# First attention: VectorE multiplies the output of two pairs back ahead of head 0's remainder; GpSimd's gates become semaphore increments

## The chip, the cores and the metric

The kernel runs on one core of a Trainium2 chip. The metric is the device time of one execution in microseconds (us), the median of several. The engines are TensorE (PE in the profile), VectorE (DVE), ScalarE (ACT), GpSimd (POOL) and SyncE (SP), which here only issues DMAs. Each takes its instructions from a queue of its own in order, and they meet only at semaphores.

## The reference

Two transformer layers in a row over `x` of 8 x 512 x 128 float32, each an attention and a mixture-of-experts network, with a layer norm after each of the four. Only the first attention is touched by the change:

```python
q, k, v = jnp.einsum('bsx,xAnh->Abnsh', input, w)      # 16 heads of 64
q = q + q_bias[:, None, :]
a = jnp.einsum('bnqh,bnkh->bnqk', q, k) * h ** (-0.5)
emb = jnp.einsum('sf,fnh->nsh', sins, positional * FREQS ** (-0.5))
pos_scores = jnp.einsum('bnqh,nvh->bnqv', q, emb) * h ** (-0.5)
a = a + relative_causal(pos_scores)
a = jax.nn.softmax(jnp.where(mask, a, NEG_INF), axis=-1)
o = jnp.einsum('bnqk,bnkh->bqnh', a, v).reshape(b, s, n * h)
out = o @ (out_kernel * (fan_in * fan_out) ** (-0.25)) + out_bias
x = _layernorm(x + out, axis=-1)
```

## The kernel before

The four parts of the program follow one another: first attention (`rel_attention_phase`, some 60 to 765 us), expert network, second attention, second expert network. The first attention walks over 8 batches and, in each, over 8 pairs of heads; `n` counts the 64 pairs, `p` is the pair in its batch, `b` the batch, `k` the parity of the pair, `h` the head in the pair. `schedule` writes the same order of pairs out for every engine: pairs 0, 1, 2 and 7 of a batch by themselves, 3 to 6 in a loop. Each engine has a `body` for a pair, and its order is written by hand; so what follows an instruction on its engine waits behind it.

To keep float32 precision with 16-bit matmuls, operands are split: a high half in float16, and a low half that is the remainder. What happens for pair `n`:

- **q and k.** TensorE projects them into PSUM; VectorE brings q out (`q_evac`, L624), ScalarE k (`k_copy`, L586). GpSimd splits each in `split` (L703): a gate (`pool_gate`, L130), a select that writes the high half (L705), and, behind a wait for that select, a subtraction that writes the low half (L708). It does so four times in a pair, `k` and `q` of head 0, then of head 1. The gate adds two constants in a column of its own that no one reads. It is the instruction that stands behind the waits for semaphores and ahead of the select. The select counts `pool_steps` up by one, and the wait inside `split` is for that count to reach `chain_n`.
- **Scores.** TensorE forms them in three PSUM banks (L483 to L486), VectorE takes the negated row maxima (`maxima`, L606), ScalarE the exponentials with their sums (`exps`, L565). The bank of head 0 is free for head 1 when ScalarE has read it, and the other way round.
- **Weights.** ScalarE writes the high half of the exponentials (`high`, L574), VectorE the remainder (`low`, L618: two inputs in SBUF, 128x1280). A DMA from SP's queue turns both round (`turn`, L406) once `low` is done.
- **Sums.** VectorE takes reciprocals (L614); SP stores them and spreads them over partitions (`store_r`, `spread_r`).
- **Output.** Two pairs later TensorE multiplies the turned weights by v (`weighted_values(n - 2)`, L502) into `pv_ps`. VectorE multiplies the result by the reciprocals into `o32` (`normalise(n - 2)`, L632; it waits for that product, for the reciprocals' DMA and for the projection before), and TensorE projects `o32` into the batch's sum (`project_out`, L519).

TensorE's order in a pair is: scores of head 0, projections of k, q and v for later use, `weighted_values(n - 2)`, scores of head 1, projection of q, `project_out(n - 2)`. ScalarE's is: `exps(0)` with `k_copy` inside, `high(0)`, the high half of v, `exps(1)`, `high(1)`. In pair 2 of a batch VectorE adds the batch before to its input (`batch_sum`) and takes its statistics (`batch_stats`), GpSimd then the reciprocal root (L136, L137); in pair 7 VectorE adds a bias (L642) and normalises (L123).

VectorE's order in a pair is the part that the change touches, with GpSimd's `split`; both are printed here.

Of the kernel before, what the change touches and what calls it, by code (L numbers as in the profile page):

```python
# [22 lines left out]
P = 128  # L23
# [104 lines left out]
def pool_gate(nc, m, rows, at=0):  # L128

    nc.gpsimd.tensor_tensor(m.gate[rows, at:at + 1], m.mhalf[rows, 0:1], m.mhalf[rows, 1:2], ALU.add)  # L130
# [154 lines left out]
def rel_attention_phase(nc, io, m):  # L285


    with ExitStack() as ctx:
# [5 lines left out]
        q32 = [sb(f"q32_{h}", [P, S], F32) for h in range(2)]  # L294
        q_h = [sb(f"q_h{h}", [P, S], F16) for h in range(2)]
        q_l = [sb(f"q_l{h}", [P, S], F16) for h in range(2)]
        k32 = sb("k32", [P, S], F32)
# [21 lines left out]
        q_mm, q_out, q_split = pair("q_mm"), pair("q_out"), pair("q_split")  # L319
        k_mm, k_out, k_split = sem("k_mm"), sem("k_out"), pair("k_split")  # L320
# [6 lines left out]
        pool_steps, turn_open = sem("ra_pool"), sem("turn_open")  # L327
# [272 lines left out]
        @block.vector  # L600
        def _(dve):
            def maxima(h, n):
                for u in range(3):
                    dve.wait_ge(s_mm[h], count(n, u))
                    for c, col in UNIT_CHUNKS[u]:
                        ins = nc.vector.tensor_reduce(nmax[h][:, c:c + 1], score_ps[u][:, col:col + P * (c + 1)],  # L606
                                                      AX.X, ALU.max, negate=True)
                    ins.then_inc(max_done[h], 1)

            def reciprocals(h, n, k):  # L610
                dve.wait_ge(exp_done[h], count(n, 2))
                if later(n, 2):
                    dve.wait_ge(r_stored, 32 * (n - 1))
                nc.vector.reciprocal(rsum[h][k][:, :], sums[h][:, :]).then_inc(r_done[h], 1)  # L614

            def low(h, n, k):
                dve.wait_ge(p_hi[h], n + 1)
                nc.vector.scalar_tensor_tensor(p16[h][k][:, 1, :], prob[h][:, :], P_SCALE, p16[h][k][:, 0, :],  # L618
                                               ALU.mult, ALU.subtract).then_inc(p_lo[h], 1)

            def q_evac(h, n, pw):
                dve.wait_ge(q_mm[h], n + 1)
                dve.wait_ge(q_split[h], n)
                nc.vector.scalar_tensor_tensor(q32[h][:, :], q_ps[:, :], m_flat(m.q_bias)[:, ds(PAIRS * h + pw, 1)],  # L624
                                               m.q_mult[:, h, :], ALU.add, ALU.mult).then_inc(q_out[h], 1)

            def normalise(n, k):
                dve.wait_ge(pv_mm, n + 1)
                dve.wait_ge(r_in, 32 * (n + 1))
                if later(n, 1):  # L630
                    dve.wait_ge(out_mm, n)
                nc.vector.tensor_tensor(o32[:, :].rearrange("p (c q) -> p c q", q=P), pv_ps[:, :].rearrange("p (c q) -> p c q", q=P),  # L632
                                        r_bc[k][:, :].rearrange("p (q c) -> p c q", c=QC), ALU.mult).then_inc(o_done, 1)

            def v_low(n, k):
                dve.wait_ge(v_hi, n + 1)
                nc.vector.scalar_tensor_tensor(v_l[k][:, :, :].rearrange("p c n -> p (c n)"), v_ps[:, :], W_SCALE,
                                               v_h[k][:, :, :].rearrange("p c n -> p (c n)"), ALU.mult, ALU.subtract).then_inc(v_lo, 1)

            def add_bias(b):  # L640
                xb = m_flat(m.x)[:, ds(b * S, S)].rearrange("p (c d) -> p c d", d=D)
                nc.vector.tensor_tensor(xb, xb, m.bo_bc[:, :].unsqueeze(1).to_broadcast([P, QC, D]), ALU.add).then_inc(bias_in, 1)  # L642

            def batch_sum(b):
                dve.wait_ge(out_mm, PAIRS * (b + 1))
                dve.wait_ge(bias_in, b + 1)
                dve.wait_ge(ln_dve, b + 1)
                nc.vector.scalar_tensor_tensor(y[:, :, :].rearrange("p c d -> p (c d)"), out_ps[:, :], O_SCALE / P_SCALE,
                                               m_flat(m.x)[:, ds(b * S, S)], ALU.mult, ALU.add).then_inc(y_done, 1)

            def batch_stats(b):
                dve.wait_ge(y_done, b + 1)
                layer_norm_stats(nc, dve, m, b, y, st, mv)

            def batch_norm(b):
                layer_norm_apply(nc, dve, m, b, y, mv, rstd,
                                 m_flat(m.x)[:, ds(b * S, S)].rearrange("p (c d) -> p c d", d=D)).then_inc(ln_dve, 1)

            def body(n, t, b, p, k):
                wrap = at(p, PAIRS - 1)  # L660
                behind = wrap and not at(b, 0)
                pw = 0 if wrap else p + 1
                maxima(0, n)
                if at(p, 2) and not at(b, 0):
                    batch_sum(b - 1)
                if later(n, 1):
                    reciprocals(1, n - 1, 1 - k)
                    low(1, n - 1, 1 - k)
                q_evac(0, n + 1, pw)
                if at(p, 2) and not at(b, 0):  # L670
                    batch_stats(b - 1)
                reciprocals(0, n, k)
                low(0, n, k)
                if later(n, 2):
                    normalise(n - 2, k)
                maxima(1, n)
                q_evac(1, n + 1, pw)
                v_low(n, k)
                if wrap:
                    add_bias(b)  # L680
                if behind:
                    batch_norm(b - 1)

            def first_front():
                vector_gate(nc, m).then_inc(ln_dve, 1)
                q_evac(0, 0, 0)
                q_evac(1, 0, 0)

            def last():
                n = B * PAIRS  # L690
                reciprocals(1, n - 1, 1)
                low(1, n - 1, 1)
                normalise(n - 2, 0)
                normalise(n - 1, 1)
                batch_sum(B - 1)
                batch_stats(B - 1)
                batch_norm(B - 1)

            schedule(dve, first_front, body, last)

        @block.gpsimd
        def _(pool):
            def split(rows, src, hi, lo, chain_n):  # L703
                pool_gate(nc, m, rows)
                nc.gpsimd.affine_select(out=hi, in_=src, compare_op=ALU.is_ge, fill=0.0, base=0,  # L705
                                        pattern=[[1, S]], channel_multiplier=0).then_inc(pool_steps, 1)
                pool.wait_ge(pool_steps, chain_n)
                return nc.gpsimd.tensor_tensor(lo, src, hi, ALU.subtract)  # L708


            def split_q(h, n):
                pool.wait_ge(q_out[h], n + 1)
                pool.wait_ge(s_mm[h], 3 * n)
                pool.wait_ge(k_split[h], n + 1)
                split(slice(0, P), q32[h][:, :], q_h[h][:, :], q_l[h][:, :], 4 * n + 2 + 2 * h).then_inc(q_split[h], 1)

            def split_k(h, n):
                if h == 0:
                    pool.wait_ge(k_out, n + 1)
                pool.wait_ge(s_mm[h], 3 * n)  # L720
                pool.wait_ge(q_split[1 - h], n + h)
                r = slice(64 * h, 64 * h + 64)
                split(r, k32[r, :], m.k_h[h][r, :], m.k_l[h][r, :], 4 * n + 1 + 2 * h).then_inc(k_split[h], 1)

            def front(n):
                for h in range(2):
                    split_k(h, n)
                    split_q(h, n)

            def body(n, t, b, p, k):  # L730
                split_k(0, n + 1)
                split_q(0, n + 1)
                split_k(1, n + 1)
                split_q(1, n + 1)
                if at(p, 2) and not at(b, 0):
                    layer_norm_gpsimd(nc, pool, m, b - 1, mv, ve, rstd)

            def last():
                layer_norm_gpsimd(nc, pool, m, B - 1, mv, ve, rstd)

            schedule(pool, lambda: front(0), body, last)
# [1200 lines left out]
def m_flat(t):  # L1942

    a = t[tuple(slice(None) for _ in t.shape)]
    names = "abcd"[:len(t.shape) - 1]
    return a if len(names) == 1 else a.rearrange(f"p {' '.join(names)} -> p ({' '.join(names)})")
# [90 lines left out]
```

## Time and profile before

| | us |
|---|---|
| median of 3 runs | 1633.0 (1631.59 to 1633.61) |
| the profiled execution | 1630.46 |
| its span, first to last instruction | 1628.7 |

Busy time over the whole span: TensorE 1351.0 us (83%), VectorE 1305.7 (80%), ScalarE 947.3 (58%), GpSimd 921.4 (57%). Between 200 and 300 us, in the middle of the first attention, it is TensorE 86.8, VectorE 91.5, ScalarE 70.9, GpSimd 87.5 of 100 us, at a granted clock of 1.00. No engine is full there. In a timeline the columns are start and duration in us, the engine, the line, the operation, output and input with their shapes, and in brackets idle time of the engine just before and what ended it. A start and a duration add up to an end; the next instruction of the engine often starts up to 0.09 us before it.

### The profile page before, as it was taken

The page shows a single profiled execution, that of the slowest core. Times are in us where ns is not written, and L with a number is a line of the kernel's source. Part 1 is how long each engine was busy: PE and PEld are TensorE (multiplying, and loading weights), DVE is VectorE, ACT ScalarE, POOL GpSimd, SP SyncE. Part 2 cuts the span into 40 slices and gives each one's busy share as a digit, 9 for nine tenths or more (in the row PEclk, how much of TensorE's full clock was granted, in tenths as well). Part 3 has the DMA queues.
Part 4 walks back from the last instruction along what each step waited for, and adds up shares of the span by engine and source line. Part 5 has one row for each costly group of instructions (what it writes and reads, how often), then busy time and mean ns, then how long its engine had stood idle before and what let it go on. Part 6 is the DMA issues. An engine that isn't in the chain of part 4 may idle for free. (4 is left out here: it accounts for less than half of the span.)

```text
span 1628.7 us, 36836 instructions
## 1 busy us (share of the span) xinstructions
PE 1351.0 (83%) x11495; PEld 775.6 (48%) x11495; DVE 1305.7 (80%) x2722; ACT 947.3 (58%) x1857; POOL 921.4 (57%) x1203
## 2 busy tenths in 40 slices
PE   4888888888988988886698987489899899997936
PEld 3466656655665656654366665123332333332316
DVE  3799899998999898996788888387777877777834
ACT  2676767776767767773244444157666666665631
POOL 2788988888898989896455555211221231231635
PEclk9899999999999999997699999599999999999978
DMA  5667766565666656564000000411011111101001
GB/s 153 136 152 144 146 145 145 129 154 134 147 145 144 144 139 148 131 147 100 1 1 1 0 0 0 150 48 37 29 35 34 35 32 30 40 27 32 25 8 33
DMA packets 401554, 133.51 MB, mean 82 GB/s; under 512 B 362156, under 2 KB 389793, under 8 KB 401377
## 3 DMA queue, kind: packets, MB, share of 16 engines
q1 hardware_dynamic: 398144, 128.41, 33.2%
q10 hardware_dynamic: 1824, 3.15, 0.6%
q0 software_dynamic: 1536, 1.34, 0.3%
q8 instruction: 26, 0.43, 0.1%
q14 instruction: 24, 0.19, 0.1%
HBM read 37.14 MB, written 13.15 MB: 31 GB/s over the span
## 5 line engine op out<-in xcount | busy, mean ns | idle before, releaser
L565 ACT ACTIVATE prob<-score_ps,nmax 128x512 f32<-128x512 f32 (+3 forms) x512 | 264.8, 525 | 202.7 <-DVE nmax L606 201.9
L1577 DVE TENSOR_REDUCE a_nm<-a_s 128x1 f16<-128x512 f32 x512 | 324.5, 687 | 52.8 <-PE a_s L1349 51.9
L1503 ACT ACTIVATE a_pt<-a_st 128x1024 f32<-128x1024 f32 x256 | 260.7, 1021 | 121.8 <-PE a_st L1367 118.7
L618 DVE SCALAR_TENSOR_TENSOR p<-prob,p 128x1280 f16<-128x1280 f32 x128 | 214.4, 1675 | 44.8 <-ACT p L574 44.8
L1349 PE MATMUL a_s<-a_kop,a_qop 128*128 128x512 f16 x512 | 198.1, 388 | 58.8 <-DVE a_nm L1577 42.3
L606 DVE TENSOR_REDUCE nmax<-score_ps 128x1 f32<-128x512 f32 (+3 forms) x512 | 217.9, 480 | 18.1 <-PE score_ps L486 15.9
L708 POOL TENSOR_TENSOR k_l<-k,k_h 64x512 f16<-64x512 f32 x130 | 191.5, 1473 | 10.9
L483 PE MATMUL score_ps<-k_h,q_h 128*128 128x512 f16 (+3 forms) x512 | 156.5, 306 | 48.5 <-ACT prob L565 28.9
L130 POOL TENSOR_TENSOR gate<-mhalf 128x1 f32<-128x1 f32 (+1 forms) x284 | 85.8, 302 | 190.5 <-ACT k L586 64.4
L708 POOL TENSOR_TENSOR q_l<-q,q_h 128x512 f16<-128x512 f32 x130 | 183.0, 1408 | 10.8
L574 ACT ACTIVATE p<-prob 128x1280 f16<-128x1280 f32 x128 | 162.6, 1271 | 8.5
L902 ACT ACTIVATE hid<-fps,b_cols 128x512 f32<-128x512 f32 x130 | 86.4, 687 | 126.6 <-PE fps L862 126.6
L998 POOL TENSOR_TENSOR hid_l<-hid,hid_h 128x512 f16<-128x512 f32 x65 | 97.1, 1494 | 105.3 <-DVE hid_h L966 105.3
L485 PE MATMUL score_ps<-k_h,q_l 128*128 128x512 f16 (+3 forms) x512 | 155.2, 303 | 0.0
L484 PE MATMUL score_ps<-k_l,q_h 128*128 128x512 f16 (+3 forms) x512 | 155.2, 303 | 0.0
L1367 PE MATMUL a_st<-a_qop,a_kop 128*128 128x512 f16 x512 | 152.1, 380 | 0.2
L1349 PEld LDWEIGHTS a_s<-a_kop,a_qop 128*128 128x128 f16 x512 | 50.5, 99 | 184.4 <-DVE a_nm L1577 151.5
L1380 PE MATMUL a_pv<-a_pt,a_vaug 128*32 128x512 f32 x1024 | 137.2, 608 | 0.7 <-ACT a_pt L1503 0.7
L502 PE MATMUL pv_ps<-pt,v_h 128*64 128x256 f16 (+1 forms) x1536 | 119.1, 259 | 1.9 <-DMA pt<-p 1.9
L1699 POOL TENSOR_TENSOR a_vaug<-a_v,a_bv 128x128 f32<-128x128 f32 x32 | 14.4, 453 | 184.1 <-PE a_pv L1380 129.8
L519 PE MATMUL out_ps<-wo,o 128*128 128x128 f32 (+1 forms) x512 | 76.7, 295 | 50.1 <-DVE o L632 50.1
L486 PE MATMUL score_ps<-causal,ident_bf 128*128 128x128 bf16 x512 | 113.2, 221 | 0.0
(328 smaller groups left out, 3319.2 us busy)
## 6 DMA issues: line engine op xcount, KB each, us to landing
r_bc<-r_parts SPq DMA_DIRECT2D x128, 128.0 KB, 2.8
a_qop<-q_parts SPq DMA_DIRECT2D x32, 128.0 KB
a_kop<-k_parts SPq DMA_DIRECT2D x128, 24.0 KB
x_tok<-in_L_attn_input_dram SPq DMA_DIRECT2D x4, 512.0 KB, 12.4
pt<-p SPq DMA_TRANSPOSE x128, 4.1
r_parts<-rsum SPq DMA_DIRECT2D x128, 2.0 KB, 2.2
e_w<-in_L_ffn_w_dram SPq DMA_DIRECT2D x1, 2048.0 KB, 8.4
q_parts<-a_q_h SPq DMA_DIRECT2D x16, 128.0 KB
```

The lines of the kernel that those rows point to most:

```text
L483: nc.tensor.matmul(o, q_h[h][:, qs], m.k_h[h][:, 0:w], start=True, stop=False)
L484: nc.tensor.matmul(o, q_h[h][:, qs], m.k_l[h][:, 0:w], start=False, stop=False)
L485: nc.tensor.matmul(o, q_l[h][:, qs], m.k_h[h][:, 0:w], start=False, stop=False)
L565: ins = nc.scalar.activation(prob[h][:, P_OFF[c]:P_OFF[c] + w], score_ps[u][:, col:col + w], ACT.Exp, bias=nmax[h][:, c:c + 1], accum_out= ...
L574: nc.scalar.activation(p16[h][k][:, 0, :], prob[h][:, :], ACT.Copy, scale=P_SCALE).then_inc(p_hi[h], 1)
L606: ins = nc.vector.tensor_reduce(nmax[h][:, c:c + 1], score_ps[u][:, col:col + P * (c + 1)], AX.X, ALU.max, negate=True)
L618: nc.vector.scalar_tensor_tensor(p16[h][k][:, 1, :], prob[h][:, :], P_SCALE, p16[h][k][:, 0, :], ALU.mult, ALU.subtract).then_inc(p_lo[h], 1)
L708: return nc.gpsimd.tensor_tensor(lo, src, hi, ALU.subtract)
L1349: nc.tensor.matmul(s_ps[k][:, :], qop[:, g, c * P:(c + 1) * P], kop[:, hh, g, :], start=True, stop=True).then_inc(s_mm[k], 1)
L1367: mm = nc.tensor.matmul(st_ps[r][:, i, :], kop[:, 2 * r + i, g, kc * P:(kc + 1) * P], qop[:, g, :], start=True, stop=True)
L1503: nc.scalar.activation(pt[kc % 2][r][:, :, :], st_ps[r][:, :, :], ACT.Exp, scale=1.0 / SC).then_inc(exp_done[r], 1)
L1577: nc.vector.tensor_reduce(nm[g % 2][:, c, hh:hh + 1], s_ps[c % 2][:, :], AX.X, ALU.max, negate=True).then_inc(max_done[c % 2], 1)
```

## The change

On VectorE `normalise(n - 2, k)` moves from behind `low(0, n, k)` to ahead of it. On GpSimd the gate in `split` is replaced with an increment of the semaphore `pool_steps` that the queue does itself; since every split now adds two to that count, the constants that the splits wait for are doubled. The gates of other parts of the program stay.

```diff
@@ -670,9 +670,9 @@
                 reciprocals(0, n, k)
-                low(0, n, k)
                 if later(n, 2):
                     normalise(n - 2, k)
+                low(0, n, k)
                 maxima(1, n)
@@ -700,8 +700,8 @@
-            def split(rows, src, hi, lo, chain_n):
-                pool_gate(nc, m, rows)
+            def split(src, hi, lo, chain_n):
+                pool.sem_inc(pool_steps, 1)
                 nc.gpsimd.affine_select(out=hi, in_=src, compare_op=ALU.is_ge, fill=0.0, base=0,
                                         pattern=[[1, S]], channel_multiplier=0).then_inc(pool_steps, 1)
                 pool.wait_ge(pool_steps, chain_n)
@@ -712,7 +712,7 @@
-                split(slice(0, P), q32[h][:, :], q_h[h][:, :], q_l[h][:, :], 4 * n + 2 + 2 * h).then_inc(q_split[h], 1)
+                split(q32[h][:, :], q_h[h][:, :], q_l[h][:, :], 8 * n + 4 + 4 * h).then_inc(q_split[h], 1)
@@ -720,7 +720,7 @@
-                split(r, k32[r, :], m.k_h[h][r, :], m.k_l[h][r, :], 4 * n + 1 + 2 * h).then_inc(k_split[h], 1)
+                split(k32[r, :], m.k_h[h][r, :], m.k_l[h][r, :], 8 * n + 2 + 4 * h).then_inc(k_split[h], 1)
```

## Rows read from the trace of the kernel before

**Rows 1.** Waits, 100 to 700 us: total us, times, longest us.

```profile
DVE p L618 <- ACT p L574: 37.1, 47, 0.9
```

**Rows 2.** Timeline, VectorE, one pair late in a batch; columns as above.

```profile
449.26 1.66 DVE L606 TENSOR_REDUCE nmax<-score_ps 128x1 f32<-128x512 f32 x4
...
454.42 1.50 DVE L618 SCALAR_TENSOR_TENSOR p<-prob,p 128x1280 f16<-128x1280 f32 x1
455.84 0.74 DVE L624 SCALAR_TENSOR_TENSOR q<-q_ps,q_bias,q_mult 128x512 f32<-128x512 f32 x1
...
457.50 1.66 DVE L618 SCALAR_TENSOR_TENSOR p<-prob,p 128x1280 f16<-128x1280 f32 x1 [0.85 <-ACT p L574]
459.09 1.06 DVE L632 TENSOR_TENSOR o<-pv_ps,r_bc 128x512 f32<-128x512 f32 x1
460.08 1.66 DVE L606 TENSOR_REDUCE nmax<-score_ps 128x1 f32<-128x512 f32 x4
```

**Rows 3.** Timeline, ScalarE, the same pair.

```profile
453.32 0.67 ACT L565 ACTIVATE prob<-score_ps,nmax 128x512 f32<-128x512 f32 x1
...
456.20 1.27 ACT L574 ACTIVATE p<-prob 128x1280 f16<-128x1280 f32 x1
```

**Rows 4.** Timeline, GpSimd, the same pair.

```profile
450.36 1.16 POOL L708 TENSOR_TENSOR q_l<-q,q_h 128x512 f16<-128x512 f32 x1
451.66 0.19 POOL L130 TENSOR_TENSOR gate<-mhalf 64x1 f32<-64x1 f32 x1
451.80 0.61 POOL L705 TENSOR_SCALAR_AFFINE_SELECT k_h<-k 64x512 f16<-64x512 f32 x1
...
453.96 0.61 POOL L705 TENSOR_SCALAR_AFFINE_SELECT q_h<-q 128x512 f16<-128x512 f32 x1
454.65 2.28 POOL L708 TENSOR_TENSOR q_l<-q,q_h 128x512 f16<-128x512 f32 x1
...
457.21 0.60 POOL L705 TENSOR_SCALAR_AFFINE_SELECT k_h<-k 64x512 f16<-64x512 f32 x1
```

**Rows 5.** Timeline, TensorE, the same pair: first score, last of `weighted_values`.

```profile
451.65 0.39 PE L483 MATMUL score_ps<-k_h,q_h 128*128 128x512 f16 x1 [1.02 <-ACT prob L565]
...
457.18 0.22 PE L502 MATMUL pv_ps<-pt,v_h 128*64 128x128 f16 x2
```

**Rows 6.** Timeline, all engines, an early pair of a batch.

```profile
405.26 1.05 DVE L632 TENSOR_TENSOR o<-pv_ps,r_bc 128x512 f32<-128x512 f32 x1
...
410.76 2.08 DVE L618 SCALAR_TENSOR_TENSOR p<-prob,p 128x1280 f16<-128x1280 f32 x1
...
412.68 0.20 POOL L130 TENSOR_TENSOR gate<-mhalf 64x1 f32<-64x1 f32 x1 [1.20 <-ACT k L586]
...
413.52 0.22 PE L502 MATMUL pv_ps<-pt,v_h 128*64 128x128 f16 x2
...
414.25 1.78 DVE L618 SCALAR_TENSOR_TENSOR p<-prob,p 128x1280 f16<-128x1280 f32 x1 [0.67 <-ACT p L574]
...
414.85 1.23 POOL L130 TENSOR_TENSOR gate<-mhalf 128x1 f32<-128x1 f32 x1 [0.17 <-POOL k_l L708]
...
415.95 1.06 DVE L632 TENSOR_TENSOR o<-pv_ps,r_bc 128x512 f32<-128x512 f32 x1
```

**Rows 7.** Timeline, VectorE, change of batch and the third pair behind it.

```profile
479.15 1.67 DVE L618 SCALAR_TENSOR_TENSOR p<-prob,p 128x1280 f16<-128x1280 f32 x1 [0.84 <-ACT p L574]
...
485.36 2.24 DVE L123 TENSOR_SCALAR x_tok<-ln_y,ln_mv,ln_rstd 128x128 f32 x4
487.52 1.67 DVE L606 TENSOR_REDUCE nmax<-score_ps 128x1 f32<-128x512 f32 x4
...
492.28 1.69 DVE L618 SCALAR_TENSOR_TENSOR p<-prob,p 128x1280 f16<-128x1280 f32 x1 [0.88 <-ACT p L574]
...
512.74 0.86 DVE L110 BATCH_NORM_STATS2 ln_st<-ln_y 128x6 f32<-128x128 f32 x4
```

**Rows 8.** Timeline, SP's queue: the transpose of head 1's weights.

```profile
456.01 2.60 SPq L406 DMA_TRANSPOSE pt<-p  x1
```

## The prediction

> **What bounds the kernel now.** I read three views, in this order: the groups of instructions and the waits of the stretch 100 to 700 us, then the timeline of one pair on each engine, then the pairs around a change of batch. The first attention has 64 pairs, so its 700 us are some 10.8 us a pair. A pair is taken here from one `maxima(0)` on VectorE to the next.
>
> The waits show idle time of VectorE before head 0's `low`: 37.1 us in 47 pairs, 0.8 in each, until ScalarE's high half is there [rows 1]. The timeline shows the in-order chain behind it: `low(0)` at 457.50, `normalise` at 459.09, `maxima(1)` at 460.08 [rows 2]. `maxima(1)` lets ScalarE go on with `exps(1)`, `high(1)`, `exps(0)`, `k_copy`, `high(0)`, which lets `low(0)` of the next pair go. So the 0.98 us of `normalise` (460.08 less 459.09) lie inside a ring ScalarE - VectorE. Its ScalarE part from `exps(0)` at 453.32 to the end of `high(0)` at 457.47 is 4.15 us [rows 3].
>
> A second ring is just as long. On GpSimd a pair is four splits: gate, select, subtract. An undisturbed one takes 2.16 us (select at 451.80 to select at 453.96), the other kind 3.25 (453.96 to 457.21), because its subtract takes 2.28 us and not 1.16 [rows 4]. The long ones lie exactly over VectorE's two `low`: the subtract issued at 454.65 ends at 456.93, which is 1.15 us after 455.78, and VectorE goes on to its next instruction at 455.84 [rows 2, 4]. So the two engines exclude one another: whichever is running a `low` or a split operation makes the other wait. Two short and two long splits are 10.82 us, the whole pair (`maxima(1)` at 449.26 and at 460.08), and in this part of the batch GpSimd never idles. TensorE's first score of the pair (451.65) starts 0.14 us after the subtract issued at 450.36 ends at 451.52 [rows 4, 5].
>
> At the start of a batch, and in all of the first one, the picture differs. GpSimd waits 1.20 us for `k_copy`, VectorE's `low(1)` falls into that idle time and pays for it with 2.08 us against 1.50, and from `normalise` at 405.26 to the next at 415.95 are 10.69 us [rows 6]. Between batches a pair takes 13.13 us (479.15 to 492.28), since the bias and the normalisation (2.24 us) come in [rows 7]. A batch is 88.6 us: by `maxima(1)` 13.13, 10.69, 10.80, 10.69 and four of 10.83.
>
> **The change part by part.**
>
> *Gates.* Four gates a pair go; each sits between the semaphore it waits for and its select, and costs the select 0.14 us (451.66 to 451.80) [rows 4]. In its place stands an increment that the queue must still run through. Bounds: nothing below, and 0.14 us above, where it costs what the gate did. The nearest row is SP's: `low(1)` ends at 455.92, and the transpose behind a wait and an increment starts at 456.01, so wait and increment together take 0.09 us [rows 2, 8]. I take 0.04, a saving of 0.10 a split and 0.4 a pair, 0 to 0.56. The Trainium skill ("Advanced Engine Details and Errata", DMA Bandwidth Details) gives a semaphore increment about one cycle on trn2; by that the saving would be 0.14 a split, an estimate, and the pair 0.16 us shorter than in my sum. No row here shows an increment alone.
>
> A gate can also be the instruction that takes the wait: 1.23 us at 414.85, where 0.19 is usual [rows 4, 6]. I book no gain for that 1.0 us. The gate waits there for VectorE's `low`, and the select behind it then meets the same `low`. The Trainium skill ("SBUF — State Buffer", SBUF: two separate sides) states the exclusion as a lock held for a full instruction, between a VectorE operation with two SBUF inputs and any GpSimd operation that reads SBUF; by it the select, with one input, waits too, and this part is worth nothing. No row here shows a select waiting for a `low`, so the other outcome is the first rival.
>
> *The move.* `normalise(n-2)` now comes before `low(0)`. It needs the product of two pairs back, whose last matmul is issued at 457.18 and ends at 457.40. VectorE is free for it at 456.6 (`low(1)` 454.42, the q evacuation at 455.84, the reciprocals) [rows 2, 5]. So in the steady pairs it starts at 457.43 and not in the idle time, and `low(0)`, queued behind it, starts at 458.41 instead of 457.50. That is 0.91 us later, and with it `maxima(1)` comes no earlier, measured from the first score: the 0.98 us leave the ring and a wait of nearly the same size for TensorE takes its place. Who waits behind: ScalarE's `exps(1)`, SP's transpose of head 0 (its queue has nothing else to do then), and TensorE's projection, which gets its input 1.7 us earlier and did not need it. At the start of a batch the product ends at 413.74, and VectorE is free at 413.58 (0.67 before 414.25) [rows 6], so there the cover is nearly right, and right after a change of batch it is complete.
>
> *The new pair.* Count from the end of head 0's subtract. TensorE starts at 0.13, its product ends at 5.90 (5.75 from 451.65 to 457.40) [rows 5]; `normalise` 5.9 to 6.9; `low(0)` from 6.9. GpSimd: each split 2.05 without its gate, so `low(1)`, at 2.90 as now (454.42 less 451.52), meets the boundary between q1's select and subtract (2.9), and `low(0)` lands in the next subtract (6.3 to 7.4) or its end. A `low` occupies 1.35 us (454.42 to 455.78). If it comes within an instruction of GpSimd the pair pays 1.0 to 1.13 (2.28 less 1.15), since the hand-over is hidden; in a gap 1.35. The pair is thus 4 x 2.05 = 8.2 plus 2.1 to 2.3: 10.3 to 10.5. I take 10.4.
>
> The ring through the new wait: 5.77 (to the end of the product) + 0.98 + `low(0)` 1.4 + 1.4 for the first maximum and the first exponential (0.67 [rows 3], the maximum about the same), together 9.6, plus what `low(0)` waits for GpSimd, at most 1.04 (a subtract just issued). That is at most 10.6, under today's 10.83. ScalarE's ring is today's 10.82 less the 0.98 that leaves it, 9.8, and may wait as long; where it does, it too ends at 10.7.
>
> *Batch change.* From `maxima(0)` after the normalisation (487.52) to `low(0)` the time is ScalarE's, and the 0.88 us of idle time take the moved instruction nearly whole. The pair goes from 13.13 to 12.1 [rows 7]: a gain of 1.0. In the third pair of a batch, `batch_sum` and `batch_stats` stand before it (512.74 on) and fill VectorE already [rows 7]; there `normalise` is only moved. With GpSimd now running closer behind, its two `low` can be blocked by 0.4 and 0.8 us where they meet nothing today: 0 to 1.4 worse, I take 0.9.
>
> *Sum.* A batch: -1.0 (change), +0.9 (third pair), and for six pairs (two of 10.69, four of 10.83, together 64.7) against 6 x 10.4 = 62.4: -2.3. Net -2.4, times 7 is -17. The first batch has no normalisation: 6 pairs from 10.70 to 10.4, -2. With rounding, -18. The profiled execution took 1630.5 us (span 1628.7 and 1.8 around it), 2.5 below the median of 1633.0; its 1612.5 stand for a median of 1615. The ends of the unknowns: pair 10.25 and third pair unharmed give -30, 1603; pair 10.6 and third pair +1.4 give -5, 1628.
>
> **The rivals.**
>
> *More comes back (chance 0.12).* If a select may run beside a `low`, head 0's `low` costs GpSimd some 0.3 and not 1.0, GpSimd falls under 9.9, and the rings of 9.6 to 10.0 decide: pair 10.0. Six pairs give -4.7, with the change of batch -5.7, times 7, and the first batch -4: about -42 with the third pair at its dearer end left out, 1591. For it: no select in these rows is long. Against it: the `low(0)` of 457.50 took 1.66 us, as if it waited for the select that ran from 457.21 to 457.81 [rows 2, 4].
>
> *The gates were not the price (0.12).* The increment and its dispatch cost what the gate did. GpSimd still needs 10.8 a pair and the moved 0.98 only turns into waits for TensorE and GpSimd. Left are -7 (batch changes) and +6 (third pairs): 1632. For it: the gate's 0.14 is dispatch, and an increment is dispatched too.
>
> *Slower (0.10).* `low(0)` now waits for `normalise`, hence for TensorE, and both `low` start in GpSimd's gaps, so each costs 1.35 instead of 1.13. That is +0.4 a pair; it decides once the gates give back less than this 0.4. With nothing given back, 48 pairs x 0.4 = 19, +10 for the third pairs, -7 for the batch changes, and the median is 1655; half way it is 1645. Against it: a `low` that starts in one gap shifts GpSimd so that the next one seldom does.
>
> **How the numbers follow.** My forecast, GpSimd-bound pairs of 10.4 us, has 0.66: 1615, own range 1603 to 1628. A measurement of this kernel can tell 0.2% from no change, 3.3 us, so the forecast and the first rival count as faster, 0.78 in all; no difference 0.12; slower 0.10. The range of 8 in 10 leaves out most of the first rival and of the slower one: 1600 to 1636.
>
> **What would show it.** Right: no gate rows; steady pairs of 10.3 to 10.5; GpSimd without idle time in nearly all pairs, the first batch included; a new wait of VectorE at `normalise` for TensorE's product, 0.3 to 0.9 us, in the place of the one at `low`; TensorE's projection no longer waiting for `normalise`; the pair at the change of batch near 12.1. Wrong: selects of 1.2 to 1.9 us that nevertheless leave 10.8 a pair, or selects unblocked beside a `low` and pairs near 10.0; the gap between subtract and select still 0.3 us (an increment as dear as the gate); `low(0)` above 2.5 us each time.

## The result

| | before | after |
|---|---|---|
| median of 12 runs each, one chip, us | 1631.39 | 1633.85 |
| ratio of after to before, 95% interval | | 1.0021 (1.0012 to 1.0029) |
| the same two kernels on another chip, 20 and 10 runs | 1632.08 | 1632.08, ratio 1.0005 (0.9994 to 1.0016) |
| span of the profiled execution | 1628.7 | 1630.1 |

The change gains nothing; on the first chip the median is 2.5 us longer. The forecast was 1615 us, 18 us less than the 1633.0 known then. Ratios here and below leave out runs that the chip slowed down; there was one, of the kernel with the third pair in the old order, at 1968 us and a mean clock of 0.65.

Where the time went is seen best pair by pair. In what follows a pair is the time between two remainders of v on VectorE (`v_low`, one in each pair), and p is its place in the batch. These are the pairs of the fifth batch, in us:

| pair | 0 | 1 | 2 | 3 | 4 | 5 | 6 | 7 | batch |
|---|---|---|---|---|---|---|---|---|---|
| before | 13.13 | 10.69 | 10.80 | 10.70 | 10.84 | 10.82 | 10.81 | 10.84 | 88.6 |
| forecast | 12.1 | 10.4 | 11.7 | 10.4 | 10.4 | 10.4 | 10.4 | 10.4 | 86.2 |
| after | 12.85 | 10.37 | 12.34 | 12.22 | 9.97 | 10.45 | 10.36 | 10.45 | 89.0 |

Six of the eight pairs became shorter, as forecast. Pairs 2 and 3 (the third and fourth of a batch) lost 1.5 us each, and that used up the whole gain. From the first to the last such mark the first attention took 696.3 us before and 697.8 after.

**Steady pairs.** Steady pairs are those late in a batch, where one pair is like the next. VectorE, after (timeline; columns as in the rows ahead of the prediction):

```profile
464.49 1.76 DVE L606 TENSOR_REDUCE nmax<-score_ps 128x1 f32<-128x512 f32 x4
...
466.25 1.46 DVE L618 SCALAR_TENSOR_TENSOR p<-prob,p 128x1280 f16<-128x1280 f32 x1
...
469.28 1.08 DVE L632 TENSOR_TENSOR o<-pv_ps,r_bc 128x512 f32<-128x512 f32 x1 [0.66 <-PE pv_ps L502]
470.28 1.80 DVE L618 SCALAR_TENSOR_TENSOR p<-prob,p 128x1280 f16<-128x1280 f32 x1
472.00 1.67 DVE L606 TENSOR_REDUCE nmax<-score_ps 128x1 f32<-128x512 f32 x4
```

GpSimd in the same pair:

```profile
465.69 0.61 POOL L705 TENSOR_SCALAR_AFFINE_SELECT q_h<-q 128x512 f16<-128x512 f32 x1 [0.26 <-POOL k_l L708]
466.39 2.34 POOL L708 TENSOR_TENSOR q_l<-q,q_h 128x512 f16<-128x512 f32 x1
468.89 0.60 POOL L705 TENSOR_SCALAR_AFFINE_SELECT k_h<-k 64x512 f16<-64x512 f32 x1 [0.16 <-POOL q_l L708]
469.57 1.15 POOL L708 TENSOR_TENSOR k_l<-k,k_h 64x512 f16<-64x512 f32 x1
470.99 1.56 POOL L705 TENSOR_SCALAR_AFFINE_SELECT q_h<-q 128x512 f16<-128x512 f32 x1 [0.26 <-POOL k_l L708]
472.63 1.15 POOL L708 TENSOR_TENSOR q_l<-q,q_h 128x512 f16<-128x512 f32 x1
```

Against [rows 2, 4]: the wait of VectorE before `low` (0.85 us for ScalarE) is gone, and `normalise` has one of 0.66 for TensorE's product. GpSimd has no gate; its select follows the subtract by 0.27 us (470.72 to 470.99) or 0.16 (468.73 to 468.89), where it was 0.28 to 0.31. Head 1's remainder at 466.25 meets the subtract of 466.39, which takes 2.34 us. Head 0's, at 470.28, meets the subtract of 469.57 and takes 1.80 us itself, and then the select of 470.99 waits for it, 1.56 us against 0.6. The waits of 100 to 700 us say the same over all pairs (total us, times, longest):

```profile
PE score_ps L483 <- POOL q_l L708: 51.2, 41, 2.0
DVE o L632 <- PE pv_ps L502: 29.9, 39, 1.4
```

The wait that [rows 1] shows no longer appears in that stretch, and TensorE waits for GpSimd's subtract 51.2 us, where it was 11.3. GpSimd is not without idle time everywhere: it waits for ScalarE's copy of k 26 times, 47.7 us in all (24 times and 34.0 before), the longest 3.69 us, at a change of batch.

**The third and the fourth pair.** VectorE, GpSimd, ScalarE and TensorE, after, in this order; the third pair of the fifth batch and its hand-over to the fourth:

```profile
421.87 2.04 DVE L618 SCALAR_TENSOR_TENSOR p<-prob,p 128x1280 f16<-128x1280 f32 x1
...
424.49 0.86 DVE L110 BATCH_NORM_STATS2 ln_st<-ln_y 128x6 f32<-128x128 f32 x4
...
425.74 1.04 DVE L632 TENSOR_TENSOR o<-pv_ps,r_bc 128x512 f32<-128x512 f32 x1
426.71 2.37 DVE L618 SCALAR_TENSOR_TENSOR p<-prob,p 128x1280 f16<-128x1280 f32 x1
```

```profile
421.40 1.16 POOL L708 TENSOR_TENSOR q_l<-q,q_h 128x512 f16<-128x512 f32 x1
...
426.57 1.16 POOL L708 TENSOR_TENSOR q_l<-q,q_h 128x512 f16<-128x512 f32 x1
427.89 1.66 POOL L705 TENSOR_SCALAR_AFFINE_SELECT k_h<-k 64x512 f16<-64x512 f32 x1 [0.16 <-issue]
```

```profile
429.71 0.69 ACT L565 ACTIVATE prob<-score_ps,nmax 128x512 f32<-128x512 f32 x1 [4.51 <-DVE nmax L606]
```

```profile
426.92 1.08 PE L519 MATMUL out_ps<-wo,o 128*128 128x128 f32 x8
430.55 0.39 PE L483 MATMUL score_ps<-k_h,q_h 128*128 128x512 f16 x1 [2.55 <-ACT prob L565]
430.77 0.58 PE L484 MATMUL score_ps<-k_l,q_h 128*128 128x512 f16 x1
431.14 0.63 PE L485 MATMUL score_ps<-k_h,q_l 128*128 128x512 f16 x1
```

Head 1's remainder comes 0.47 us after the subtract of 421.40 was issued and takes 2.04; head 0's comes 0.14 us after that of 426.57 and takes 2.37. Both take 1.46 when nothing is in the way, so 1.5 us are lost (0.58 and 0.91), and nothing in this pair has room for them: VectorE is busy in all of it (12.30 of 12.34 us below). ScalarE stood for 4.51 us, TensorE for 2.55. Then TensorE's matmuls over 512 columns take 0.6 us instead of 0.38. The stretches of the second to fifth pair (columns: the stretch, its length; busy time and number of instructions of TensorE, its weight loads, VectorE, ScalarE and GpSimd; granted clock as a share; DMA share and GB/s):

```profile
408.54:418.91 10.37, 9.26 (x98) 6.73 (x97) 9.64 (x18) 7.69 (x22) 9.20 (x9) 1.00 0.67 158
418.91:431.25 12.34, 9.79 (x100) 6.86 (x99) 12.30 (x27) 7.69 (x22) 10.19 (x10) 0.98 0.56 128
431.25:443.47 12.22, 10.84 (x99) 7.52 (x98) 10.20 (x17) 7.91 (x22) 9.26 (x10) 0.88 0.57 129
443.47:453.44 9.97, 9.09 (x97) 6.60 (x96) 9.24 (x17) 7.70 (x22) 6.91 (x7) 1.00 0.67 158
```

TensorE's busy time in the fourth pair is the point: the same matmuls were busy 10.84 us and not 9.1 to 9.3, at a mean clock of 0.88. In 432 to 434 us the granted clock was 0.50, 1.2 GHz of 2.4. Before, it is 1.00 in every pair of this batch.

**Change of batch.** The bias of the last pair, VectorE, and what GpSimd does meanwhile, after:

```profile
485.30 1.49 DVE L642 TENSOR_TENSOR x_tok<-x_tok,bo_bc 128x512 f32 x1
```

```profile
485.09 1.16 POOL L708 TENSOR_TENSOR k_l<-k,k_h 64x512 f16<-64x512 f32 x1
```

The bias took 0.79 to 0.87 before and takes 1.49 or 1.50 in all eight batches now. It too has two inputs in SBUF, and it now comes while GpSimd subtracts.

### The profile page after: what moved, and what is told of

Read it like the earlier page. It is cut to its first block and busy times, and to the rows that moved or that the text cites. A ratio compares the mean times of both kernels' runs of the same rounds, so it can differ in the third digit from the quotient of the medians.

```text
span 1630.1 us, 36711 instructions
## 1 busy us (share of the span) xinstructions
PE 1345.2 (83%) x11495; PEld 782.9 (48%) x11495; DVE 1315.1 (81%) x2722; ACT 942.1 (58%) x1857; POOL 881.2 (54%) x943
## 5 line engine op out<-in xcount | busy, mean ns | idle before, releaser
L708 POOL TENSOR_TENSOR q_l<-q,q_h 128x512 f16<-128x512 f32 x130 | 191.9, 1476 | 10.8
L485 PE MATMUL score_ps<-k_h,q_l 128*128 128x512 f16 (+3 forms) x512 | 158.6, 310 | 0.0
L708 POOL TENSOR_TENSOR k_l<-k,k_h 64x512 f16<-64x512 f32 x130 | 151.4, 1164 | 10.8
L705 POOL TENSOR_SCALAR_AFFINE_SELECT q_h<-q 128x512 f16<-128x512 f32 x130 | 130.6, 1005 | 41.3 <-POOL k_l L708 30.2
L705 POOL TENSOR_SCALAR_AFFINE_SELECT k_h<-k 64x512 f16<-64x512 f32 x130 | 96.3, 741 | 98.0 <-ACT k L586 79.5
L483 PEld LDWEIGHTS score_ps<-k_h,q_h 128*128 128x128 f16 x512 | 51.0, 100 | 142.6 <-ACT prob L565 60.5
## 6 DMA issues: line engine op xcount, KB each, us to landing
x_tok<-in_L_attn_input_dram SPq DMA_DIRECT2D x4, 512.0 KB, 12.3
```

Of the source, the lines that this page charges most:

```text
L483: nc.tensor.matmul(o, q_h[h][:, qs], m.k_h[h][:, 0:w], start=True, stop=False)
L485: nc.tensor.matmul(o, q_l[h][:, qs], m.k_h[h][:, 0:w], start=False, stop=False)
```

## The experiments

My theory behind them (A) was: GpSimd and VectorE exclude one another. The gain of the steady pairs is real, and the loss sits in the third pair, where both remainders fall on subtracts, and in the fourth, through TensorE's clock. The rival theories were that the increments give nothing or harm (B), and that the fourth pair's loss has to do with GpSimd's normalisation or the delayed chain. Ratios are to the kernel before on the same chip; after itself stands at 1.0021 and 1.0005. It shared a chip with only three of its variants (statistics last, bias moved, zeros in the first pair); the others are compared with it by their ratios. "Marks" are the first attention from first to last mark in the profiled execution.

| kernel | ratio (95%) | marks, us |
|---|---|---|
| before | 1 | 696.3 |
| after | 1.0021 (1.0012 to 1.0029) | 697.8 |
| after, again | 1.0005 (0.9994 to 1.0016) | 695.7 |
| move only | 1.0028 (1.0015 to 1.0040) | 699.9 |
| increments only | 0.9999 (0.9989 to 1.0008) | 694.8 |
| after, third pair in the old order | 0.9956 (0.9941 to 0.9971) | 687.5 |
| after, matmuls of zeros in the third pair | 0.9990 (0.9975 to 1.0004) | 690.4 |
| after, statistics last in the third pair | 1.0001 (0.9989 to 1.0013) | 698.3 |
| the same, matmuls of zeros in nearly all pairs | 0.9950 (0.9934 to 0.9967) | 684.7 |
| old third pair and bias in the second pair | 0.9954 (0.9934 to 0.9974) | 690.2 |
| old third pair and matmuls of zeros in the first | 0.9931 (0.9913 to 0.9949) | 684.3 |
| the last two together | 0.9924 (0.9907 to 0.9941) | 686.4 |
| after, GpSimd's subtractions cut short (work left out), one run | 0.971 | 653.5 |

### The two halves of the change

The move without the increments:

```diff
                 reciprocals(0, n, k)
-                low(0, n, k)
                 if later(n, 2):
                     normalise(n - 2, k)
+                low(0, n, k)
```

> The move alone, gates as before. Theory A (the loss sits in the third and fourth pair of a batch, where the moved instruction puts both remainders of VectorE behind GpSimd's subtracts and lets TensorE's clock fall; the gain of the other pairs is GpSimd's, and comes mostly from the gates): steady pairs 10.7 us instead of 10.83, third and fourth pair about 3 us longer together, so about 2 us a batch over before: 1640 to 1648, slower than both kernels. Theory B (the move is what gains in the other pairs, and the increments give nothing or harm): steady pairs 10.4 as in the changed kernel, total at or below 1634.

The increments without the move (the other part of the diff):

> The increments alone, normalise behind the remainder as before. Theory A: the third and fourth pair stay at 10.8 and 10.7 us, the clock stays at 1.00; the steady pairs are held by the ring ScalarE - VectorE and gain 0 to 0.3 us each: 1620 to 1631. Theory B (increments give nothing): 1631 within 2; if they harm, above 1634.

Measured: 1.0028 and 0.9999. Steady pairs took 10.74 us with the move alone, 10.5 to 10.6 with the increments alone, and 10.4 with both. So in the steady pairs the increments give 0.2 to 0.3 us and the move 0.1 to 0.2; theory B falls there. The move alone has the same loss in the third pair, 11.85 us. Behind it there are two cases. In three of the seven later batches the clock fell (0.86 to 0.88) and the fourth pair took 11.4 us. In the other four the clock stayed at 1.00 and the fourth pair took 10.0, but the fifth took 12.1:

```profile
177.35:189.45 12.10, 9.45 (x98) 6.85 (x99) 10.01 (x18) 8.06 (x22) 11.00 (x15) 1.00 0.81 128
```

There GpSimd runs the two operations of its normalisation (L136 and L137, 1.45 and 1.04 us) ahead of its splits, and TensorE waits 2.31 us for the subtract behind them. So the rival theory holds for these four batches: time is lost there without any fall of the clock. The total came out lower than I had expected (about 5 us over before, not 8 and more). One reason is its change of batch of 11.98 us, where the bias met no subtract:

```profile
488.89 0.67 DVE L642 TENSOR_TENSOR x_tok<-x_tok,bo_bc 128x512 f32 x1
```

The increments alone gain 0.2 us in most pairs and give them back at the change of batch, which theory A had not foreseen. TensorE waits 2.72 us there for `normalise`, still in its old place, and its clock falls to 0.93 in two pairs (13.92 and 11.14 us against 13.13 and 10.69):

```profile
404.40 1.88 PE L519 MATMUL out_ps<-wo,o 128*128 128x128 f32 x8 [2.72 <-DVE o L632]
```

```profile
392.60:406.52 13.92, 10.96 (x99) 7.40 (x100) 13.04 (x22) 7.80 (x22) 9.53 (x10) 0.93 0.50 114
406.52:417.66 11.14, 10.66 (x100) 7.10 (x99) 9.51 (x18) 8.02 (x22) 8.05 (x9) 0.93 0.62 143
```

### The third pair in the old order

```diff
                 reciprocals(0, n, k)
+                if at(p, 2):
+                    low(0, n, k)
                 if later(n, 2):
                     normalise(n - 2, k)
-                low(0, n, k)
+                if not at(p, 2):
+                    low(0, n, k)
```

> The changed kernel with the old order in the third pair of each batch only (normalise behind the remainder there). Theory A: third pair back from 12.3 to 10.8 us, fourth back from 12.2 to about 10.5 since TensorE keeps its full clock: 3.0 x 7 = 21 us less than the changed kernel, 1611 to 1617. Rival (the fourth pair's loss comes from the normalisation's GpSimd operations or from the new order elsewhere, not from the third pair): only the 1.5 us of the third pair come back, 1622 to 1625, or the loss moves to another pair and nothing comes back.

Measured 0.9956, marks 10.3 us under those of after. In the fifth batch:

```profile
414.71:426.15 11.44, 10.03 (x101) 6.85 (x99) 11.40 (x27) 7.69 (x22) 9.75 (x10) 1.00 0.71 160
426.15:436.75 10.60, 9.14 (x97) 6.60 (x96) 10.16 (x18) 7.69 (x22) 9.51 (x10) 1.00 0.53 125
```

Both pairs recover, the fourth wholly (10.60, clock 1.00), the third to 11.44 in four batches and to 10.8 in the three others. About half of the expected 21 us came. The rest stayed for three reasons. The third pair still has one blocked remainder (2.04 us and 1.46) where it takes 11.44. In three batches the clock now fell in the second pair (12.33, 11.61 and 12.34 us at 0.86 to 0.88, against 10.36). And the fifth pair, which took 9.96 behind the long fourth one, is back at 10.37.

### TensorE kept busy

Eleven matmuls of zeros times zeros are added to the output bank in the third pair, behind the projection:

```diff
+                if at(p, 2):
+                    for _ in range(11):
+                        nc.tensor.matmul(out_ps[:, :], m.zeros[:, 0:P], m.zeros[:, :], start=False, stop=False, skip_group_check=True)
```

> The changed kernel with eleven matmuls of zeros times zeros added to the output bank behind the projection in the third pair (they add 0, about 2.4 us of TensorE's 2.7 us of idle time). Theory A (the fourth pair is long because TensorE's granted clock falls to 0.5 after that idle time): clock stays at 1.00, the fourth pair goes from 12.2 to about 10.7, the third stays at 12.3: 1.5 x 7 = 10 us less than the changed kernel, 1621 to 1626. Rival (the fourth pair is late for another reason, GpSimd's two normalisation operations or the delayed chain): no change or longer, 1632 to 1636.

Fifth batch, second to fourth pair; before them TensorE's row of the added work:

```profile
424.91 2.54 PE L549 MATMUL out_ps<-zeros 128*128 128x512 f16 x11
```

```profile
403.77:416.10 12.33, 11.13 (x99) 7.63 (x98) 10.55 (x17) 7.96 (x22) 9.58 (x10) 0.86 0.58 133
416.10:427.82 11.72, 11.72 (x110) 7.87 (x109) 11.68 (x27) 7.69 (x22) 8.11 (x8) 1.00 0.57 135
427.82:437.78 9.96, 9.16 (x98) 6.60 (x96) 9.23 (x18) 7.69 (x22) 8.94 (x9) 1.00 0.70 159
```

The fourth pair took 10.0 us in all seven batches instead of 11.4 to 12.3, and its clock stayed at 1.00. Useless work of 2.5 us in a pair made the next one 1.4 to 2.3 us shorter. That shows the clock as the cause: in two of the batches the third pair was as long as in after (12.33 us), and GpSimd's normalisation was still in the fourth pair (here its L137 even took 2.25 us, against 1.01 in after). It was not worth the expected 10 us (marks 7.4 under those of after) since in four batches the clock now fell in the second pair, where I had added nothing.

### The statistics at the end of the third pair

```diff
-                if at(p, 2) and not at(b, 0):
-                    batch_stats(b - 1)
                 reciprocals(0, n, k)
...
                 v_low(n, k)
+                if at(p, 2) and not at(b, 0):
+                    batch_stats(b - 1)
```

> The changed kernel with batch_stats moved in the third pair from ahead of head 0's part to the end of the pair. Theory A (in the third pair the 1.2 us of statistics stand between head 1's remainder and normalise, so head 0's remainder comes late and behind a GpSimd subtract, and TensorE then idles until its clock falls): third pair 10.6 to 11.4 us instead of 12.3, fourth 10.5 instead of 12.1, clock 1.00: 2.0 to 3.0 us a batch less, 14 to 21 us under the changed kernel. Rival (VectorE's total work fills the third pair anyway): the 1.2 us appear at the end of the pair, and only the clock's share, 10 us at most, comes back.

The fifth pair: rows of GpSimd and TensorE from the sixth batch, and the stretch of the fifth.

```profile
523.67 1.45 POOL L136 TENSOR_TENSOR ln_ve<-ln_mv,ln_eps 128x4 f32<-128x4 f32 x1
525.20 1.01 POOL L137 TENSOR_TENSOR ln_rstd<-ln_ve,mhalf 128x4 f32<-128x4 f32 x1
...
526.86 2.35 POOL L708 TENSOR_TENSOR k_l<-k,k_h 64x512 f16<-64x512 f32 x1
```

```profile
531.38 0.39 PE L483 MATMUL score_ps<-k_h,q_h 128*128 128x512 f16 x1 [2.48 <-POOL q_l L708]
```

```profile
441.02:454.79 13.77, 11.63 (x101) 7.77 (x101) 10.69 (x18) 8.15 (x22) 10.89 (x11) 0.88 0.51 120
```

The third pair shrank to 10.30 and the fourth to 10.40, as theory A had it. Yet the ratio was 1.0001: the fifth pair took 13.75. GpSimd's two normalisation operations, 2.5 us together, came in front of its splits; TensorE waited 2.48 us for the subtract, and the clock fell once more (0.88, in all seven batches). Both theories were partly wrong: the loss is not tied to the third and fourth pair, and GpSimd's normalisation can cause it as well. To test this, six matmuls of zeros went into nearly all pairs of that kernel:

```diff
+                if closed(b, p) and p == 0 or not isinstance(p, int) or p >= 2:
+                    for _ in range(6):
+                        nc.tensor.matmul(out_ps[:, :], m.zeros[:, 0:P], m.zeros[:, :], start=False, stop=False, skip_group_check=True)
```

> The statistics at the end of the third pair, with six matmuls of zeros (they add 0, 1.3 us) behind TensorE's projection in all pairs but the second of a batch. Theory A (the fifth pair's 13.75 us there are again TensorE's clock, fallen after 2.5 us of idle time that the normalisation's GpSimd operations make): clock 1.00 in it, 12.2 us, first attention 8 to 11 us shorter than with the statistics at the end alone, 0.993 to 0.995 of the kernel before. Rival (the filler delays the scores in pairs without idle time): 10.4 us pairs grow to 10.6 or more, and nothing is gained.

Ratio 0.9950: the fifth pair 11.78, clock 1.00 in all pairs from the second batch on, the steady ones unchanged at 10.4 to 10.5. So 2.0 us of the 13.75 were the clock's, and the 1.4 us left over a steady pair came at the full clock, with the normalisation ahead of the splits. From the third batch on the added matmuls, busy 1.46 us in a pair, made no other pair longer, but for the sixth (10.45 us and not 9.98), which no longer follows a slowed one.

### After, once more, and two versions meant to be faster

> The changed kernel itself, beside its variants on one chip. Expected 1.001 to 1.003 times the kernel before, with third and fourth pairs of 12.3 and about 12.1 us in each batch and TensorE's clock below 1.00 in the fourth.

Ratio 1.0005: within 0.2% of before. In one of seven batches the clock did not fall and the fourth pair took 9.99 us, in the six others it took 11.3 to 12.3.

The bias in the second pair, over the old third pair:

```diff
-                if wrap:
+                if at(p, 1):
                     add_bias(b)
```

> The third pair in the old order, as in the run before with that, and add_bias moved from the last pair of a batch to the second. Theory A (its 1.49 us at the change of batch, against 0.8 alone, are a wait for GpSimd's subtract): the change of batch goes from 12.85 to 11.4 us, the second pair from 10.4 to 11.2 or 11.9: 0 to 4 us less than with the third pair alone. Rival: the second pair takes all of it and more, since VectorE has no idle time there: 0 to 5 us more.

The change of batch fell by 0.66 us, to 12.19, not by 1.4. The ratio, 0.9954, is no different from that without the move of the bias (0.9956): the clock now fell in all seven batches, in five at the second pair (11.4 to 12.3 us) and in two at the fourth, where it had fallen in three.

Eight matmuls of zeros in the first pair, over the old third pair:

```diff
+                if closed(b, p) and p == 0:
+                    for _ in range(8):
+                        nc.tensor.matmul(out_ps[:, :], m.zeros[:, 0:P], m.zeros[:, :], start=False, stop=False, skip_group_check=True)
```

> The third pair in the old order, and eight matmuls of zeros (they add 0, 1.7 us) behind TensorE's projection in the first pair of each batch. Theory A (where the second pair of a batch took 11.6 to 12.3 us instead of 10.4, TensorE's clock had fallen after its idle time in the first): no clock below 1.00 from the second batch on, second pairs all 10.4 us, 3 to 5 us less than with the third pair alone. Rival (those pairs are long for another reason, and the filler only delays the scores): second pairs stay at 12.3, or all get longer.

```profile
389.39:402.24 12.85, 11.81 (x107) 7.29 (x106) 12.85 (x22) 7.80 (x22) 8.15 (x9) 1.00 0.51 120
402.24:412.61 10.37, 9.26 (x98) 6.74 (x97) 9.63 (x17) 7.69 (x22) 9.20 (x9) 1.00 0.68 158
```

As expected: second pairs of 10.37 from the third batch on, the first pair no longer than before the filling, clock 1.00 from the second batch on. The added matmuls are busy 1.89 us a batch. The ratio is 0.9931; its interval still overlaps that of the kernel without them (0.9956), and the marks are 3.2 us shorter. On its chip this kernel beats before and after by 0.7% each. With the bias moved too:

> The third pair in the old order, the eight matmuls of zeros in the first pair, and add_bias moved to the second pair. Theory A: change of batch 12.2 instead of 12.86, second pair 10.4 without a fall of the clock, third 11.5: 0.5 us a batch, 3 to 5 us less than with the first two alone, 0.990 to 0.992 of the kernel before. Rival: the bias delays the second pair's remainders behind GpSimd's subtracts, 0 to 5 us more.

0.9924, which cannot be told from 0.9931. Its marks are 2 us longer: the third pair takes 12.19 in all seven batches, and in four of them the clock fell in it (0.94 to 0.96) and in the fourth pair. So the move of the bias adds nothing that these runs show.

### Less work on GpSimd

```diff
-                return nc.gpsimd.tensor_tensor(lo, src, hi, ALU.subtract)
+                return nc.gpsimd.tensor_tensor(lo[:, 0:64], src[:, 0:64], hi[:, 0:64], ALU.subtract)
```

(The low halves of q are also set to 0 once before the first pair.)

> The changed kernel with GpSimd's subtraction in split cut from 512 to 64 columns (the rest of the low halves of q and k stays as it was: work left out, about 1.0 us of each of four subtractions a pair). Theory A (GpSimd's splits and VectorE's remainders exclude one another, and GpSimd bounds the steady pairs): no remainder over 2.0 us, the third pair about 1 us shorter or more, steady pairs at the next bound, 9.3 to 10.0 us. Rival (VectorE's order or TensorE's product bounds the steady pairs whatever GpSimd does): steady pairs stay at 10.4.

One execution, 1598.4 us against 1646.9 before on its chip. VectorE's remainders (duration in ns, shortest, median, longest), and the third and a steady pair:

```profile
L618 DVE SCALAR_TENSOR_TENSOR p<-prob,p x128: 1451/1467/1609, 46.2 to 705.9; 128x1280 f16<-128x1280 f32 x128
```

```profile
396.96:407.74 10.78, 9.65 (x100) 6.79 (x98) 10.74 (x27) 7.67 (x22) 4.73 (x8) 1.00 0.61 146
...
417.79:427.80 10.01, 9.46 (x99) 6.69 (x97) 9.28 (x17) 7.69 (x22) 3.93 (x8) 1.00 0.69 157
```

No remainder took over 1.61 us, the third pair took 10.78 and not 12.34, the change of batch 10.93 and not 12.85, no clock fell from the second batch on, and the steady pairs took 10.01 to 10.06. That is theory A on each point but the last: the steady pairs lie just above the expected 9.3 to 10.0, so the next bound is only 0.4 us below GpSimd's. The edit shortens a subtract from 1.15 to 0.30 us and so lets TensorE's scores begin earlier too; what it shows of the exclusion alone is the remainders' durations.

## Why the prediction was wrong

**Right.** The two exclusive engines and GpSimd as the bound of the steady pairs: 10.36 to 10.45 us, forecast 10.3 to 10.5. `normalise` waits for TensorE's product, 0.57 to 0.74 us in nearly all steady pairs, in the place of the wait at `low`. The gate's increment: a split saves 0.05 or 0.12 us, 0.34 a pair, taken as 0.4. No gain was booked for the gates of 1.2 us, and indeed the select behind them now waits for the remainder. The Trainium skill ("SBUF — State Buffer", SBUF: two separate sides) says that the lock holds against any GpSimd operation that reads SBUF, and the trace agrees: selects with their one input took up to 1.92 us beside a remainder, 0.61 otherwise. With that the rival in which a select runs beside a remainder has fallen. One sign of being right came only in part: GpSimd still waits for ScalarE's copy of k at the change of batch (3.69 us) and in the early pairs.

**Wrong: the step "batch change", and the sum's silence on TensorE's clock.** A batch was to take 86.2 us and took 89.0. The 2.8 us between them are:

- Fourth pair, +1.8 (10.4 forecast, 12.22 measured). The forecast counted it among six equal pairs and kept TensorE's durations as the trace of before has them, at a clock of 1.00. The stall of the third pair was in my sum, but I gave it only its own length. It left TensorE without work for 2.55 us, and the first matmuls behind it ran at half clock. Keeping TensorE busy there brought the fourth pair to 10.0.
- Third pair, +0.6 (11.7 and 12.34). The mechanism was forecast, two blocked remainders, with 0 to 1.4 us; I took 0.9, and it measured 1.54, a little over the upper end (the remainders were held up by 0.58 and 0.91, priced at 0.4 and 0.8).
- Change of batch, +0.75 (12.1 and 12.85). The moved instruction did go into the idle time, but the bias behind it, which the sum did not name, met a subtract and took 0.63 us more. With the move alone it met none, and that pair took 11.98, near the forecast.
- The other five pairs, -0.4: the fifth took 9.97, 0.4 under a steady pair. It does so only behind a long fourth pair; behind one of 10.0 it takes 10.4.

The first batch was to give 2 us and gave none: its third pair took 15.57 us instead of 13.52. There `normalise` waited for the reciprocals' DMA, and head 0's remainder, at 71.34 before, stood behind it until 75.31:

```profile
74.32 1.08 DVE L632 TENSOR_TENSOR o<-pv_ps,r_bc 128x512 f32<-128x512 f32 x1 [5.02 <-DMA r_bc<-r_parts]
75.31 1.50 DVE L618 SCALAR_TENSOR_TENSOR p<-prob,p 128x1280 f16<-128x1280 f32 x1
```

The text ahead of the prediction names three things that `normalise` waits for, the reciprocals' DMA among them. The prediction priced TensorE's product only.

**The rivals.** "Slower" asked for both remainders in GpSimd's gaps in the steady pairs. That did not happen; the loss of about 3 us in two pairs of each batch was not in it. "The gates were not the price" gave the nearest time, 1632, by luck: its reason did not hold, since the increments do gain in the steady pairs.

**Open.** Which batches lose their clock differs between executions of nearly the same schedule: six of seven in the fourth pair in the second profile of after, three of seven in the second pair with the old third pair. What decides it in a single batch is not settled here. The kernel before has it too, once: in its seventh batch the clock fell at the change of batch (0.90) and the next pair took 10.96 us and not 10.70. That the bias costs 0.63 us a batch was seen in rows, and moving it shortened the change of batch by 0.66, but no difference of the whole kernel could be measured.

## What to carry to other kernels

Where an in-order schedule is tightened, look at the exceptional iterations (a batch's change, its statistics) separately. An instruction moved into an idle slot of the regular ones may find none there, and its stall passes to other engines. If the stall leaves TensorE idle for some 2 us, price what follows at the lower clock also, and try to fill the gap with matmuls that change nothing: here 1.46 us of zeros in nearly all pairs went with a ratio of 0.9950, where it was 1.0001 without them. And name for each instruction of VectorE with two SBUF inputs what GpSimd is doing at that moment; a saving anywhere shifts these meetings.

## What the runs showed of the hardware

- TensorE's granted clock fell to 0.50 behind idle times of 2.48 to 2.72 us (statistics last; after; increments only), but also of 2.02 (old third pair, fourth batch), 1.90 (the last two together, fourth batch) and 1.66 us (move only, fifth batch). It stayed at 1.00 behind 2.28 to 2.32 us (move only, fifth pair, in four batches) and behind 2.49 or 2.50 (before, at five of six changes of batch; at the other it fell). Move only had the same idle time of 1.66 us ahead of the fourth pair in seven batches, and the clock fell in three of them. So the length of the idle time before it does not say it.
- A fall made the fourth pair of after 1.4 to 2.3 us longer (11.4 to 12.3 against 10.0 without one) and the fifth with the statistics last 2.0 (13.75 and 11.78). With the increments only it began at the end of one pair, and the next took 11.14 and not 10.6.
- A matmul over 512 columns took 0.38 us at the full clock, 0.58 to 0.63 right after the fall.
- A semaphore increment on GpSimd's queue in place of a gate on a 128x1 or 64x1 column shortened the way from a subtract to the next select from 0.31 to 0.26 us behind the subtract of k, and from 0.28 to 0.16 behind that of q.
- The bias on VectorE, 128x512 with two inputs in SBUF, took 0.67 to 0.87 or 1.49 us, according to what GpSimd was doing.
